# Attention parts stored head by head in DRAM, and second buffers for projected keys and queries in two of three stages

## What is computed

```python
q = (layernorm(x) @ Wq + bq)        # 16 heads of 16
k, v = (ctx @ Wk + bk), (ctx @ Wv + bv)
w = softmax(mask(einsum('bhqd,bhkd->bhqk', q, k) * scale))
x = x + einsum('bhqk,bhkd->bhqd', w, v).reshape(B, S, D) @ Wo + bo
```

## Time and profile before

| | us |
|---|---|
| median of 3 runs | 4700.8 (4699.31 to 4715.89) |
| the profiled execution | 4706.52 |
| its span | 4704.8 |
| PE busy in it | 3914.7 (83%) |
| DVE busy | 3099.6 (66%) |
| ACT busy | 2060.3 (44%) |
| POOL busy | 796.3 (17%) |
| DMA queue of SP, share of 16 engines | 20.4% |

### The profile page before, as it was taken

How to read it: one execution, slowest core, us unless ns; L and a number is a source line. 1 busy time by engine, 2 the same in 40 slices (tenths; PEclk the granted TensorE clock), 3 DMA queues, 4 the chain that set the end, 5 groups by cost and what they waited for, 6 DMA issues and landing times. The chain is left out here.

```text
span 4704.8 us, 82799 instructions
## 1 busy us (share of the span) xinstructions
PE 3914.7 (83%) x30525; PEld 2826.9 (60%) x30525; DVE 3099.6 (66%) x7110; ACT 2060.3 (44%) x3636; POOL 796.3 (17%) x510
## 2 busy tenths in 40 slices
PE   6599999699367999785499996669988974999899
PEld 5244444588365777674388885535555663455577
DVE  7466664546656666545466664668867884988687
ACT  2155555134113333342154443247776851677511
POOL 4333330501341000000023323210000021000000
PEclk8699999599668999897599998869998997899999
DMA  6333331201320000010244545412210024121100
GB/s 205 102 98 101 101 96 41 88 21 44 106 77 32 18 18 18 28 43 31 72 126 123 130 125 144 166 60 66 67 37 14 1 71 148 55 66 65 34 19 19
DMA packets 202874, 337.94 MB, mean 72 GB/s; under 512 B 26036, under 2 KB 119781, under 8 KB 202566
## 3 DMA queue, kind: packets, MB, share of 16 engines
q1 hardware_dynamic: 186680, 306.61, 20.4%
q0 software_dynamic: 15888, 27.23, 2.8%
HBM read 242.42 MB, written 107.01 MB: 74 GB/s over the span
## 5 line engine op out<-in xcount | busy, mean ns | idle before, releaser
L1904 ACT ACTIVATE a_pT<-a_psS 128x512 f32<-128x512 f32 x1536 | 835.9, 598 | 405.0 <-PE a_psS L1790 399.6
L1976 DVE TENSOR_REDUCE a_mx<-a_psA 128x1 f32<-128x512 f32 x1024 | 656.6, 685 | 88.1 <-PE a_psA L1768 87.8
L1768 PE MATMUL a_psA<-a_ks,a_qs 48*128 48x512 f32 (+1 forms) x1536 | 404.4, 522 | 160.9 <-PEq L46 59.0
L1805 PE MATMUL a_psZ<-a_pT,a_V 128*17 128x128 f32 x12288 | 488.4, 278 | 0.0
L1972 DVE CUSTOM_DVE_ANT_0 a_scored<-a_psA,a_hide_q 128x512 bf16<-128x512 f32 x512 | 332.6, 688 | 193.4 <-PE a_psA L1768 192.3
L1805 PEld LDWEIGHTS a_psZ<-a_pT,a_V 128*17 128x17 f32 x12288 | 272.6, 97 | 270.8 <-issue 161.7
L1768 PEld LDWEIGHTS a_psA<-a_ks,a_qs 48*128 48x128 f32 (+1 forms) x1536 | 151.2, 192 | 408.7 <-issue 176.0
L1790 PE MATMUL a_psS<-a_qs,a_ks 50*128 50x512 f32 (+1 forms) x1536 | 319.1, 409 | 3.2 <-ACT a_pT L1904 0.8
L3244 DVE SCALAR_TENSOR_TENSOR ex_h<-ex_psU,ex_ub,ex_sg 128x512 f32<-128x512 f32 x129 | 96.9, 751 | 188.6 <-PE ex_psU L159 181.6
L1988 POOL TENSOR_TENSOR X<-X,a_osb 128x512 f32<-128x512 f32 x48 | 61.2, 1280 | 941.1 <-ACT a_osb L1891 923.1
L3190 ACT CAST ex_w_h<-X 128x1024 fp32r<-128x1024 f32 x102 | 106.1, 1041 | 149.3 <-DMA X<-in_L_ffn_gw 145.3
(11 more groups left out here) (606 smaller groups left out, 10257.4 us busy)
## 6 DMA issues: line engine op xcount, KB each, us to landing
a_k_parts<-a_p_kp SPq DMA_DIRECT2D x96, 256.0 KB
a_q_parts<-a_p_qp SPq DMA_DIRECT2D x96, 256.0 KB
a_qs<-a_q_parts SPq DMA_DIRECT2D x192, 128.0 KB
a_ks<-a_k_parts SPq DMA_DIRECT2D x192, 128.0 KB
X<-in_L_ffn_gw SPq DMA_DIRECT2D x36, 512.0 KB, 4.5
X<-in_L_ffn_up_w SPq DMA_DIRECT2D x36, 512.0 KB, 3.3
X<-in_L_ffn_down_w SPq DMA_DIRECT2D x36, 512.0 KB, 3.8
top_rows<-blank_rows SPq DMA_DIRECT2D x32, 514.0 KB, 11.3
```

What stands on the lines that cost most here:

```text
L1768: nc.tensor.matmul(psA[:, unit(a, par) % 3], qs[r, g % ring, p % 2, q * P:(q + 1) * P], ks[r, g % ring, p % 2], start=True, stop=True).the ...
L1805: last = nc.tensor.matmul(psZ[q * VP:q * VP + VW, g % 2, j * P:(j + 1) * P], V[:, b, kt, g % NG * GH + j, :], pT[:, p % 2, par, kt, q * P: ...
L1904: nc.scalar.activation(pT[:, p % 2, par, kt, :], psS[:, unit(t, par) % 3], ACT.Exp).then_inc(exp_done, 1)
L1976: nc.vector.tensor_reduce(mx[:, p // 2 % 2, par, p % 2, q:q + 1], psA[:, unit(a, par) % 3], AX_X, ALU.max).then_inc(a_used, 1)
```

## The change

`q_parts` and `k_parts` are laid out part, batch, head, feature, token. A store then writes 128 rows that lie one behind another, and a load of two heads takes, for each of 16 features, two runs of 2 KB. `load_group` fills every block of 16 rows with a DMA of its own, six per `par` instead of four, without a broadcast. In attentions 2 and 3 `kp` and `qp` have two buffers, with a semaphore for each; attention 0, which has the masks, keeps one.

```diff
-def resident_projections(nc, A, G, nm, w, q_scale, q_dram, k_dram, V, wo, bo, prepare):
+def resident_projections(nc, A, G, nm, w, q_scale, q_dram, k_dram, V, wo, bo, buffers, prepare):
...
-        kp, qp = sb("kp", [P, 2, KD, S], F32R), sb("qp", [P, 2, KD, S], F32R)
+        kp, qp = sb("kp", [P, buffers, 2, KD, S], F32R), sb("qp", [P, buffers, 2, KD, S], F32R)
...
-                            heads = dram[n, :, m * P // DH:(m + 1) * P // DH].rearrange("d h t -> h d t")
+                            heads = dram[n, m * P // DH:(m + 1) * P // DH].rearrange("h d t -> (h d) t")
                             sp.dma_start(heads, parts[:, n, m].bitcast(F32)).then_inc(stored, 16)
...
-                    store(kp, k_dram[:, b], k_stored)
+                    store(kp[:, b % buffers], k_dram[:, b], k_stored[b % buffers])
                     sp.wait_ge(q_low, b + 1)
-                    store(qp, q_dram[:, b], q_stored)
+                    store(qp[:, b % buffers], q_dram[:, b], q_stored[b % buffers])
                     if b == 4:
-                        sp.wait_ge(k_stored, 64 * b)
-                        sp.wait_ge(q_stored, 64 * b)
+                        for stored in k_stored + q_stored:
+                            sp.wait_ge(stored, 64 * b // buffers)
...
-                    if b >= 1:
-                        act.wait_ge(stored, 64 * b)
+                    if b >= buffers:
+                        act.wait_ge(stored[b % buffers], 64 * (b // buffers))
...
-    LOADS = 2 * (4 + (added is not None))
+    LOADS = 2 * (6 + (added is not None))
...
-        q_dram = nc.dram_tensor(nm + "q_parts", [2, B, DH, H, S], F32).ap()
-        k_dram = nc.dram_tensor(nm + "k_parts", [2, B, DH, H, S], F32).ap()
+        q_dram = nc.dram_tensor(nm + "q_parts", [2, B, H, DH, S], F32).ap()
+        k_dram = nc.dram_tensor(nm + "k_parts", [2, B, H, DH, S], F32).ap()
...
-                    return dram[part:part + 1, b, :, first:first + 2].rearrange("r d h t -> r d (h t)")
-
-                for stack, start, src in ((qs, 0, heads(q_dram, 0).to_broadcast([2, DH, 2 * S])), (qs, 2 * DH, heads(q_dram, 1)),
-                                          (ks, 0, heads(k_dram, 1)), (ks, DH, heads(k_dram, 0).to_broadcast([2, DH, 2 * S]))):
-                    rows = slice(64 * par + start, 64 * par + start + src.shape[0] * DH)
-                    sp.dma_start(stack[rows, slot].bitcast(F32).rearrange("p j t -> p (j t)"), src).then_inc(group_loaded[slot], 16)
+                    return dram[part, b, first:first + 2].rearrange("h d t -> d h t")
+
+                for stack, third, src in ((qs, 0, heads(q_dram, 0)), (qs, 1, heads(q_dram, 0)), (qs, 2, heads(q_dram, 1)),
+                                          (ks, 0, heads(k_dram, 1)), (ks, 1, heads(k_dram, 0)), (ks, 2, heads(k_dram, 0))):
+                    rows = slice(64 * par + third * DH, 64 * par + (third + 1) * DH)
+                    sp.dma_start(stack[rows, slot].bitcast(F32), src).then_inc(group_loaded[slot], 16)
...
-        resident_projections(nc, A, G, nm + "p_", w, q_scale, q_dram, k_dram, V, wo, bo,
+        resident_projections(nc, A, G, nm + "p_", w, q_scale, q_dram, k_dram, V, wo, bo, 1 if hidden is not None else 2,
```

More of the change, by code:

```diff
@@ L1369, in resident_projections @@
         cT_h, cT_l = sb("cT_h", [P, 2, KD, S], F32R), sb("cT_l", [P, 2, KD, S], F32R)
-        kp, qp = sb("kp", [P, 2, KD, S], F32R), sb("qp", [P, 2, KD, S], F32R)
+        kp, qp = sb("kp", [P, buffers, 2, KD, S], F32R), sb("qp", [P, buffers, 2, KD, S], F32R)
         w_loaded = {n: sem(n + "_loaded") for n in names}
         w_high, w_low, small_loaded, scaled = sem("w_high"), sem("w_low"), sem("small_loaded"), sem("scaled")
-        cT_loaded, k_stored, q_stored = [sem("cT_loaded0"), sem("cT_loaded1")], sem("k_stored"), sem("q_stored")
+        cT_loaded, k_stored, q_stored = [sem("cT_loaded0"), sem("cT_loaded1")], [sem(f"k_stored{n}") for n in range(buffers)], [sem(f"q_stored{n}") for n in range(buffers)]
         cT_high, cT_low, k_in_psum, v_in_psum, q_in_psum, v_taken, k_high, k_low, q_high, q_low = (
@@ L1406, in _ @@
                     sp.wait_ge(k_low, b + 1)
-                    store(kp, k_dram[:, b], k_stored)
+                    store(kp[:, b % buffers], k_dram[:, b], k_stored[b % buffers])
                     sp.wait_ge(q_low, b + 1)
-                    store(qp, q_dram[:, b], q_stored)
+                    store(qp[:, b % buffers], q_dram[:, b], q_stored[b % buffers])
                     if b == 4:
-                        sp.wait_ge(k_stored, 64 * b)
-                        sp.wait_ge(q_stored, 64 * b)
+                        for stored in k_stored + q_stored:
+                            sp.wait_ge(stored, 64 * b // buffers)
                     prepare.loads(sp, b)
-                sp.wait_ge(k_stored, 64 * B)
-                sp.wait_ge(q_stored, 64 * B)
+                for stored in k_stored + q_stored:
+                    sp.wait_ge(stored, 64 * B // buffers)
                 sp.wait_ge(small_loaded, 16 * len(smalls))
@@ L1466, in high_part @@
                     act.wait_ge(in_psum, b + 1)
-                    if b >= 1:
-                        act.wait_ge(stored, 64 * b)
+                    if b >= buffers:
+                        act.wait_ge(stored[b % buffers], 64 * (b // buffers))
                     for m in range(KD):
-                        nc.scalar.activation(parts[:, 0, m, :], ps[:, m, :], ACT.Identity, bias=bias[:, m:m + 1]).then_inc(done, 1)
+                        nc.scalar.activation(parts[:, b % buffers, 0, m, :], ps[:, m, :], ACT.Identity, bias=bias[:, m:m + 1]).then_inc(done, 1)
                 f.scalar_roots(act, 0)
@@ L1505, in low_part @@
                         dve.wait_ge(high_done, 2 * b + m + 1)
-                        last = nc.vector.scalar_tensor_tensor(parts[:, 1, m, :], ps[:, m, :], bias[:, m:m + 1],
-                                                              parts[:, 0, m, :].bitcast(F32), ALU.add, ALU.subtract)
+                        last = nc.vector.scalar_tensor_tensor(parts[:, b % buffers, 1, m, :], ps[:, m, :], bias[:, m:m + 1],
+                                                              parts[:, b % buffers, 0, m, :].bitcast(F32), ALU.add, ALU.subtract)
                     last.then_inc(done, 1)
```

## The result

The changed kernel takes **4562.3 us** (median of 4 runs, 4558.6 to 4576.6) against 4702.5 us for the kernel before on the same chip: a ratio of 0.970, with a 95% interval of 0.967 to 0.973, or 140 us less. The forecast was 4594 us, with a range of 4562 to 4650. The profiled execution took 4560.4 us, its span is 4558.6 us; that is 146.2 us under the span of before, and the two traces are compared on that.

The account below looks back on a forecast made before the run. Stores on 8 and broadcasts on 2 DMA engines were taken to bound the projection stages. Gains of 40 + 37 + 30 = 107 us, with nothing for the score loops, gave 4594 us from the 4700.8 us median; range 4562 to 4650.

Parts of the forecast that it names:

- the cheap bound of every term: Range's lower end, 4562 us: the largest gain of the three stages, 127 us, plus 12 us of the score loops.
- The reading of the earlier trace: Projection stages: stores run on 8 DMA engines, broadcast loads on 2, some 25 GB/s each; the new shapes use 16.
- the second buffers at nothing: Attentions 2 and 3: second key and query buffers hardly needed once stores land in some 5 us; no gain counted.
- Attention 2: 40 forecast: Its projection stage goes from 155.0 to 115 us, 40 us less; 31 to 46 by its bounds.
- attention 3: 37: Its projection stage, with 14 DMAs a group and 3.3 us more of SP: 37 us less, between 28 and 43.
- the prediction's parts: Attention 2's projections: up to issue of batch 4's query stores (68.7 us), SP's issue from there, the rest to the next stage.
- DVE at 11.1 us a batch: Projection stages: DVE's work is the next limit, bringing a batch down to 11.1 us from 11.64 between statistics instructions.
- Attention 0: 30 forecast: Its projections, with masks landing sooner and a shorter tail: 30 us less, between 20 and 38.
- Score loops: 0 forecast, 12 as bound: Loops behind the projections: PE's waits for group loads, 6.6 + 5.9 us, counted as no gain, 12 us at most.
- C: Rival: DRAM writes hold at some 200 GB/s however many engines write; about 50 us gained, 4650 us; chance 0.09.
- A: Rival: new shapes don't spread over engines, only the second buffers work; 16 and 4 us gained, 4681 us; chance 0.07.
- B: Rival: SP's issue of the added loads slows the score loops of attentions 2 and 3; 4835 us; chance 0.04.

Follow-up runs that it names:

- stores on 8: Changed kernel with an unused 2 KB row behind each head's rows in DRAM, so a store's outermost size is the eight heads: ratio 0.984, 4635.4 us.
- loads on 2: Changed kernel with the duplicated high parts of a group loaded by broadcasts of one head each, still twelve DMAs a group: ratio 0.985, 4638.0 us.
- one buffer: Changed kernel with one buffer each for projected keys and queries in all three attention stages: ratio 0.972, 4570.0 us.
- loads halved: Changed kernel with each group load cut in two, 24 loads of 32 KB in place of 12 of 64 KB: ratio 0.995, 4682.3 us.

## Why the forecast was right, and where it was off

The mechanism was right, and the size was short: 107 us forecast, 140 measured. That 4562.3 still lies inside the range is luck, for it is 0.3 us from its lower end, and that end had been set by adding up the cheap bound of every term.

- **The reading of the earlier trace rows** (8 engines for stores, 2 for broadcasts) and **the second buffers at nothing** are shown, by "stores on 8", "loads on 2" and "one buffer". Undone one by one, stores give back 65.0 us of the stages, loads 41.7, the second buffers nothing (the stages are some 2.5 us shorter without them). That is 107 of the 122.5. Effects undone one at a time need not add up to the whole, and the rest was not traced. Added to the kernel before, the buffers brought 6.7 us of the stages, 1.4 of it in attention 0, whose code was then as before.
- **Attention 2: 40 forecast, 42.4 measured; attention 3: 37 and 42.4.** The mechanism held: DVE for the batches, then SP without a gap. The term mis-sized was SP's issue. In the prediction's parts attention 2 was 68.7 + 41.5 + 4.7 us, and became 71.2 + 36.7 + 4.7. I took 3.1 us for four stores and 0.54 for a load, both from queues of before; from batch 4 on they are 1.8 to 3.1, and 0.45 to 0.7. The first part came 2.5 us later than forecast and hid half of that. For attention 3 I added 3.3 us of issue for the added row; its loads issue in 0.3 us each and SP's run, 37.4 us, is only 0.7 longer than in attention 2. That is why attention 3 was the further off. The prediction's bound for cheap issue in attention 2 was 46 us.
- **DVE at 11.1 us a batch** was 10.9.
- **Attention 0: 30 forecast, 37.7 measured.** The first mask's wait ended 13.3 us sooner (11.5 forecast), the second's 22.3 (18), and DVE's last query part began 22.9 us sooner (18); from the start of that part to the next stage it now takes 7.4 us, where 22.1 us had passed, 14.7 less (12.4). The 7.7 us that were missing come from several terms: the first mask load went out 1.1 us sooner than I had it, SP came to the second 1.6 sooner, the two loads took 6.3 and 7.1 us from issue to use where I had 7 and 8 (1.6 together), and the end was 2.3 shorter (the last four stores issue in 1.8 us, not 3.1, and the next stage starts 4.2 behind them, not 5.2). Some 1 us is left over.
- **Score loops: 0 forecast, 12 as bound, 17.9 in the two traces.** I took the waits of the earlier trace rows as free, as DVE was late too; in "loads on 2" they come back with some 8 and 4 us in two loops, in "loads halved" with much more. So these waits were not free. That is shown for about 12 us; of the rest, attention 2's 4.6 is within what this loop differs by among kernels with plain loads of 64 KB (438.5 to 446.5).
- **9.0 us are not the change's.** The last stage took 262.0 to 274.6 us over the profiled runs of the fourteen kernels above, which all have it unchanged; the trace after is near the short end.
- **Rivals.** C is refuted: stores moved at 381 to 408 GB/s. A is refuted by the same rows, and its price for the buffers (20 us) was too high: 7.5 us by the ratio, 5.3 of it in the two stages that have them. B did not come to pass, but "loads halved" shows its mechanism at 24 loads a group: SP's 13.8 us set the group. With 12 loads at 0.45 us it needs 6.7 of 12.6 us.
- The Trainium skill, *DMA: Bandwidth & Descriptors*, section "Rules for kernel authors", advises to coalesce many small transfers, since under 64 KB one pays mostly overhead. Weighed in the prediction, the page's 0.95 us for 64 KB gave an estimated 11.4 us for twelve loads in a row. Their issue took 5.6 us in the score loops here, so it did not speak against the split at 64 KB; at 32 KB the trace agrees with it, since a load of 32 KB costs SP what one of 64 KB does, 0.45 us.

The sum, 107 for 140: 15.5 us missing in the stages (SP's issue price above all, then the masks), some 12 to 18 in the loops, and no more than scatter of untouched stages besides.

## What to carry to other kernels

Before adding a buffer against a wait for a DMA, look at the DMA share while only that transfer runs. Here 0.50 and 0.13 meant half and an eighth of the engines, and the outermost size was what to change. When splitting a broadcast into plain loads to spread it, count the issues on their queue at 0.45 to 0.65 us each against the loop's period; that price did not fall from 64 to 32 KB. When one engine sets the first part of a stage and a queue the rest, price them as a sum. DVE relieved by 1.0 us a batch gave 6.3 us, all ahead of the point where SP's unbroken run begins; 5.4 us taken from that run gave 1 to 2, because the rest of the stage grew by most of it.

## What the runs showed of the hardware beyond that

**One GpSimd instruction holds up one VectorE instruction.** The four instructions that write `xn` in a batch take 0.41 us each, except one. In the changed kernel, between 2947 and 2952 us (ns, min/median/max):

```profile
L215 DVE TENSOR_SCALAR a_p_xn<-X,a_p_meanvar,a_p_rstd x4: 408/410/2484, 2947.8 to 2948.8; 128x256 f32<-128x256 f32 x4
```

And POOL in the same stretch:

```profile
2948.66 2.47 POOL L1493 TENSOR_TENSOR a_p_cT_l<-a_p_cT,a_p_cT_h 128x1024 fp32r<-128x1024 f32 x1 [8.42 <-ACT a_p_cT_h L1460]
```

The last of the four began at 2948.8, just after POOL's, and ended with it at about 2951.2. The Trainium skill, *SBUF — State Buffer*, section "SBUF: two separate sides", states an exclusive lock on a port pair that VectorE and GpSimd share, in which the later one fully blocks; it names it for VectorE instructions in a two-port mode or with two SBUF inputs. The trace agrees: 2.48 us for 0.41, and 1.38 for 3.46 with the context off GpSimd. In which mode this instruction runs, no run shows.

**The price of an issue depends on the queue's state more than on the bytes.** Four stores of 256 KB went out in 1.8 us with room, in 1.8 to 3.1 from batch 4 on, in 3.3 to 6.1 in attention 2 of "stores on 8", and in up to 8.4 before the change. With room a store of 256 KB costs SP 0.45 us, as much as a load of 64 or 32 KB.
